# A graph layer on one core: GpSimd starts a group's gathers only after the previous group's have landed

## The reference

```
for l in range(2):
    xn = layernorm(x);  pos = xn @ Wpos + bpos + deg * Wdeg + bdeg;  xp = xn + pos
    q, k, v = (xp @ W + b) for Wq, Wk, Wv          # 8 heads of 16
    att   = clip(sum(q[dst] * k[src]) / 4, -50, 50)
    alpha = softmax of att over the edges of one dst
    x = x + segment_sum(v[src] * alpha, dst) @ Wo + bo
    x = x + gelu(layernorm(x) @ W1 + b1) @ W2 + b2
out = layernorm(x_in + x)
```

## Time and profile before

| what | value |
|---|---|
| median of 3 runs | 2100.44 us (2098.3 to 2102.22) |
| profiled execution: span from first to last instruction | 3221.0 us |
| PE busy / DVE busy / ACT busy / POOL busy in it | 1677.5 / 1445.7 / 910.1 / 1486.6 us |
| indirect DMAs on GpSimd | 1564, 1482.8 us, 948 ns each |
| moved by the gathers' queue (q0) | 205.10 MB |
| granted TensorE clock, mean | 0.694 |

### The profile page before, as it was taken

How to read it: one execution, slowest core, us unless ns; L and a number is a source line. 1 busy time by engine, 2 the same in 40 slices (tenths; PEclk the granted TensorE clock), 3 DMA queues, 4 the chain that set the end, 5 groups by cost and what they waited for, 6 DMA issues and landing times.

```text
span 3221.0 us, 44116 instructions
## 1 busy us (share of the span) xinstructions
PE 1677.5 (52%) x11693; PEld 1432.5 (44%) x11694; DVE 1445.7 (45%) x2484; ACT 910.1 (28%) x1616; POOL 1486.6 (46%) x1584
## 2 busy tenths in 40 slices
PE   7444444355566556555343534444456565556545
PEld 5344334345455445444333433343445454545444
DVE  8634434344444535454363434343444444434435
ACT  3212212123333323332131212122233233323322
POOL 0545444545444444544534445444544444444452
PEclk9667676767666777775666767676677667666667
DMA  2423333323323333333323333233333333333332
GB/s 74 136 85 109 95 99 97 105 93 113 97 95 105 108 99 96 114 105 97 116 72 101 102 95 107 90 102 98 102 103 104 103 93 98 110 98 99 101 119 75
DMA packets 120301, 322.97 MB, mean 100 GB/s; under 512 B 31459, under 2 KB 43684, under 8 KB 120170
## 3 DMA queue, kind: packets, MB, share of 16 engines
q0 software_dynamic: 75072, 205.10, 21.5%
q1 hardware_dynamic: 44292, 115.07, 10.7%
q10 hardware_dynamic: 838, 1.60, 0.2%
HBM read 313.45 MB, written 9.73 MB: 100 GB/s over the span
## 4 chain that ended last, share of the span: by engine, by line
another core or an unknown queue 29%; DVE 21%; issue 20%; PE 15%; DVEq 11%; ACT 2%; ACTq 0%; DMA 0%; POOL 0%; POOLq 0%
PE ps L1352 8%; DVE dots L1082 5%; DVEq L359 4%; PE ps L1337 4%; DVE msg L1106 4%; DVE prod L1072 3%; DVEq L393 2%; DVE hot L992 1%; DVEq L992 1%; DVE acc L987 1%; PE ps L1314 1%; DVEq L987 1%; DVE not_nan L1084 1%; DVE q_parts L839 1%
## 5 line engine op out<-in xcount | busy, mean ns | idle before, releaser
L566 POOL DMA_INDIRECT kv<-kv_tab,src_idx x1564 | 1482.8, 948 | 1697.8 <-DVE msg L1106 1131.3
L1352 PE MATMUL ps<-msg,hot 128*128 128x136 f32 x3896 | 783.3, 366 | 766.4 <-DVE acc L987 459.0
L1352 PEld LDWEIGHTS ps<-msg,hot 128*128 128x128 f32 x3896 | 705.0, 264 | 827.5 <-issue 531.8
L1337 PE MATMUL ps<-q_parts,hotT 128*128 x5844 | 545.4, 251 | 608.3 <-issue 436.6
L1337 PEld LDWEIGHTS ps<-q_parts,hotT 128*128 x5844 | 449.5, 113 | 717.5 <-issue 700.3
L1072 DVE TENSOR_TENSOR prod<-kv,ps 128x1024 f32<-128x1024 f32 (+1 forms) x198 | 238.1, 1202 | 608.3 <-remote 431.3
L705 ACT ACTIVATE hotT<-dist 128x1024 bf16 x246 | 259.9, 1057 | 535.0 <-remote 388.1
L992 DVE SCALAR_TENSOR_TENSOR hot<-dst_col,neg_base,ps 128x1024 f32<-128x1024 f32 (+1 forms) x246 | 311.8, 1267 | 144.4 <-issue 141.0
L702 ACT ACTIVATE dist<-dst_rows,neg_node 128x1024 bf16<-128x1024 int32 x246 | 282.4, 1148 | 146.1 <-issue 135.5
L987 DVE TENSOR_TENSOR acc<-acc,ps 128x136 f32 x246 | 71.3, 290 | 553.7 <-remote 316.1
L1082 DVE TENSOR_REDUCE dots<-prod 128x64 f32<-128x1024 f32 (+1 forms) x198 | 238.8, 1206 | 33.3 <-DVE prod L1072 24.2
(11 more groups left out here) (215 smaller groups left out, 995.4 us busy)
## 6 DMA issues: line engine op xcount, KB each, us to landing
dst_rows<-in_dst SPq DMA_DIRECT2D x194, 512.0 KB
kv<-kv_tab,src_idx POOLq DMA_INDIRECT x1564
kv_tab<-qkv SPq DMA_DIRECT2D x25, 128.0 KB
kv_tab<-qkv SPq DMA_DIRECT2D x3, 768.0 KB, 3.8
out_tab<-z SPq DMA_DIRECT2D x24, 64.0 KB
out<-out_tab SPq DMA_DIRECT2D x1, 1498.5 KB, 7.2
hot<-in_L_gnn_W SPq DMA_DIRECT2D x2, 256.0 KB
w<-in_L_gnn_W SPq DMA_DIRECT2D x2, 256.0 KB
```

The costliest lines, as they stand in the source:

```text
L566: pool.indirect_dma_start(kv[:, u, c, :], None, kv_tab[l][:, :], bass.IndirectOffsetOnAxis(ap=src_idx[:, c, at(g)], axis=0)).then_inc(kv_i ...
L1337: last = MM(qd[:, c * P:(c + 1) * P], hotT[:, bass.ds(pr % 2, 1), c * P:(c + 1) * P], q_parts[:, at(t), k * D:(k + 1) * D], start=first an ...
L1352: last = MM(agg, hot[:, u % 2, c, :], msg[:, u % 2, c, :], start=(c == 0), stop=(c == nch - 1))
```

## The change

A wait is added to GpSimd's loop: before the gathers of group g, all of group g - 1's must have landed, that is, the semaphore of its buffer must have its full count. It stands behind the wait for a free buffer. Nothing else changes: the same 1564 gathers, in the same order, into the same buffers.

```diff
@@ -562,6 +562,8 @@
                         pool.wait_ge(msg_done[l], g - SLOTS + 1)
                     elif l == 0 and g == SLOTS - 1:
                         pool.wait_ge(npair_ready, 1)
+                    if g:
+                        pool.wait_ge(kv_in[l][(g - 1) % SLOTS], 16 * (GC * ((g - 1) // SLOTS) + chunks_of(g - 1)))
                     for c in range(chunks_of(g)):
                         pool.indirect_dma_start(kv[:, u, c, :], None, kv_tab[l][:, :],
                                                 bass.IndirectOffsetOnAxis(ap=src_idx[:, c, at(g)], axis=0)).then_inc(kv_in[l][u], 16)
```

## The result

| kernel | median | runs | profiled span |
|---|---|---|---|
| before | 2099.48 us (2098.3 to 2102.22) | 4 | none at this speed |
| after | 2563.66 us (2560.73 to 2565.37) | 4 | 2561.5 us, mean granted clock 0.746 |

The ratio is 1.221 [1.2193, 1.2227]. The change costs 464 us where I forecast 345. The direction and the bound were right. The time lies 24 us above the upper end of my range.

The account below looks back on a forecast made before the run. GpSimd's gather issue was taken as the bound. 2100.4 us plus 347.8 (196 waits x 1.81 = 354.8, less 7) gave 2448, or 2434 if 14 us of compute were covered; forecast 2445, range 2380 to 2540 us.

Parts of the forecast that it names:

- sum of 2086 us: Kernel before if GpSimd never waits for a buffer: start, gathers, pauses, layer turn and end total 2086.0 us, 14.4 under the median.
- Hidden: Rival: the added wait disappears in GpSimd's idle time, no change, about 2100 us; chance 0.04.
- hidden in part: Rival: a compute-bound middle stage takes up its waits; only 100 x 1.81 = 181 us shows, 2280 us; chance 0.07.
- faster: Rival: gathers issue quicker with the queue drained each group, 2097 us at best; chance 0.01.
- Price of one wait: At a group's start, GpSimd pauses 2.11 us instead of 0.30, so each added wait costs 1.81 us.
- issue end to the last packet: First piece of a landing wait: from the last gather's issue end until its transfer's last busy slice, 1.48 us.
- last packet to the count: Second piece of a landing wait: from the transfer's last packets to its counted landing, 0.35 us.
- count to GpSimd's next start: Third piece of a landing wait: from the counted landing to GpSimd's next gather, 0.28 us.
- give-back at the turn: At each layer's last two groups, later landings remove VectorE's 3.5 us delay, twice: -7 us.
- signs I named: Profile after: group starts at least 2.1 us after last issue, releaser DMA or unknown; 1.25 us steps within groups; span nearly unchanged.
- More than forecast: Rival: at most groups the `dst_rows` load delays the last gather's landing; 2650 us, or about 2560 and more; chance 0.05.
- recording holds some engine back: Profiled execution of before: its 3221.0 us, 1.53 times the 2100.44 us median, was put down to profiling.

Follow-up runs that it names:

- e_swap4: Kernel after with its two waits swapped, landing wait written first, on a chip where before takes 2099.35 us: 2448.26 us, ratio 1.1659.
- e_lag2: Kernel before plus a wait for the landing of group g - 2, nearly always met, on a slow chip: 3180.97 us, ratio 0.9982.
- e_both: Kernel before plus landing waits before each group's first gather (landing written first) and fifth gather, on the 2099 us chip: 3065.04 us, ratio 1.4591.
- b_again: Kernel before, unchanged, built anew and profiled on a slow chip: 3183.34 us timed, profiled run 3153.3 us with a span of 3151.4.
- e_after2: Kernel after, unchanged, run on a slow chip beside the kernel before: 2660.49 us against 3181.97, ratio 0.8354.
- e_swap: Kernel after with its two waits swapped, landing wait written first, on a slow chip: 2675.1 us against 3183.34 for before, ratio 0.8402.
- e_pause4: Kernel before plus one scratch-tile write by GpSimd before every fourth gather, no landing wait, on a slow chip: 3149.84 us, ratio 0.9919.
- e_half: Kernel before gathering only four of eight chunks from group 4 on (output differs), on a slow chip: 1980.09 us, ratio 0.6231.
- e_midonly: Kernel before plus a landing wait only before each group's fifth gather, for its first four, on a slow chip: 2587.97 us, ratio 0.8131.
- e_pause8: Kernel before plus five scratch-tile writes by GpSimd at each group's start, no landing wait, on the 2099 us chip: 2463.07 us, ratio 1.1733.

## Why the prediction was wrong, and where it was right

**The bound.** Right. The sum of 2086 us named GpSimd's issue from durations alone, and the added waits came out in the time almost one for one: 464 us more, of which the trace gives 505.9 - 195 x 0.30 = 447 us to landing waits. "Hidden", "hidden in part" and "faster" were refuted on the chip of the forecast: no wait for a free buffer is left in the kernel after.

**Price of one wait.** This term failed: I took 2.11 us for the pause at a group's start, measured 2.59 us. Of its three pieces, "issue end to the last packet" and "last packet to the count" held together: 1.76 us to landing in the chain (2.71 - 0.95), VectorE starting after 1.92, forecast 1.83. (One of the two was misread: the last busy slice of the earlier trace rows ends at 130.5 us, not 130.6, so by that row it is 1.38 us in place of 1.48, and the forecast would have been 20 us lower.) The failed piece is "count to GpSimd's next start: 0.28 us". It came from the earlier trace rows. Two waits stand before that gather too, L554 for the table and L555 for `cols_read`, but there the late one is written first; ScalarE had met L555 at 23.9 us. That is the order of `e_swap4`. In the change the one written last is the one that is not met: 0.74 us. I wrote that "the waits add no issue worth counting", from groups whose one wait had long been met; `e_lag2` shows that this is true of met waits (0.305 us), and it does not carry over to a separate one that isn't. `e_swap4` is the control. The same two waits in the other order give pauses of 2.12 us and 2448 us in all. What differs is shown by the rows there: the separate wait stands 12.0 us before its gather where it is met early, and 0.72 us before it where it is the landing. What fills this 0.7 us is not shown.

**The sum of the kernel after**, term by term, against its span:

| term | forecast | measured |
|---|---|---|
| until the first gather | 87.0 | 87.0 |
| 1564 gathers | 1482.8 | 1483.4 |
| pauses within groups | 1366 x 0.30 = 409.8 | 441.0 |
| landing waits | 196 x 2.11 = 413.6 | 505.9 |
| turn of the layers (105.3 less the first wait, 82.1) | 21.0 | 23.2 |
| after the last gather (2561.5 - 2539.3 - 0.95) | 19.6 | 21.2 |
| sum | 2433.8 | 2561.7 |

The span is 2561.5. So 92.3 us of the miss are the landing waits and 31.2 us the pauses within groups. The second has two parts: 22 us in the 14 late second gathers, and 9 us because the usual pause is a little over 0.30 us, which I had rounded. In `e_swap4` the late gathers are 14 as well, but of 0.45 us: 418.4 us in place of 441.0. So this part too hangs on the order of the waits; its cause stays open. The two together are the difference between the kernel after and `e_swap4`: 90.3 + 22.6 = 112.9 us, and the medians are 115.4 apart.

The 14.4 us between my sum for before and its median stay partly open, since no trace of before at 2099 us exists: the rounding of the short pauses accounts for 6 to 9 of them.

**The give-back at the turn** (7 us) was not measured by itself; the two terms that hold it, the turn and the end, came out 2.2 and 1.6 us above the forecast. The signs I named held nearly throughout: a group starts over 2.1 us after the last issue with a DMA as the releaser (three starts of 196, behind one wait, are just under), and the steps inside a group are 1.25 us. The rise of more than 450 us, which I had tied to later landings, came without them.

**The upper end.** "More than forecast" rested on the `dst_rows` load. At group starts it is mostly not in the way, as I argued: `e_swap4` has 2.12 us in the mean, and in the kernel after the load was issued 4 to 7 us before the last gather at 176 of the 196 starts. `e_both` shows longer pauses with that load, in the middle of a group, and somewhat above the bound that I gave (3.46 us a pause, against 2.8 + 0.3). I had a cause above the forecast and gave it the upper end of the range; the cost that came was another, of the order of two waits, and had no bound in my range at all. A row that could have warned was in the trace of before: at the turn of the layers a separate wait, L408, stands just ahead of the gather of the earlier trace rows, which starts at 1660.23, 0.8 us later.

```profile
L408 POOLq EVENT_SEMAPHORE  x1: 17/17/17, 1659.4 to 1659.4; - x1
```

I had taken the whole turn as 18.9 us and not looked into it.

**The profiled execution.** Wrong. I forecast its span within 2% of 3221 us; it is 2561.5. The step that failed is "recording holds some engine back". `b_again` shows profiled and timed runs alike. I had taken two speeds of the same program for a difference between profiled and timed. The second step failed too: at the slow speed, where GpSimd idles over 1000 us, I had these pauses take the waits up and the span stay, and it fell to 2658.4 us (`e_after2`).

**What holds the kernel before on the other chips.** This was a faster case that I did not see (my rival of that name had another reason), though the trace ahead shows it. TensorE in the kernel before, slow speed (start, duration, instruction, [idle before]):

```profile
191.08 0.27 PE L1337 MATMUL ps<-q_parts,hotT 128*128 x1 [1.85 <-issue]
192.50 0.26 PE L1337 MATMUL ps<-q_parts,hotT 128*128 x1 [1.15 <-issue]
193.91 0.26 PE L1337 MATMUL ps<-q_parts,hotT 128*128 x1 [1.14 <-issue]
196.00 0.27 PE L1337 MATMUL ps<-q_parts,hotT 128*128 x1 [1.83 <-issue]
...
200.18 3.99 PE L1352 MATMUL ps<-msg,hot 128*128 128x136 f32 x16
204.97 2.09 PE L1352 MATMUL ps<-msg,hot 128*128 128x136 f32 x16 [0.80 <-DVE acc L987]
207.54 1.73 PE L1337 MATMUL ps<-q_parts,hotT 128*128 x24 [0.47 <-issue]
```

GpSimd at the same time:

```profile
195.64 0.95 POOL L566 DMA_INDIRECT kv<-kv_tab,src_idx  x1 [0.30 <-issue]
213.34 0.94 POOL L566 DMA_INDIRECT kv<-kv_tab,src_idx  x1 [16.75 <-DVE msg L1106]
```

And VectorE:

```profile
204.53 0.29 DVE L987 TENSOR_TENSOR acc<-acc,ps 128x136 f32 x1 [19.88 <-PE ps L1352]
```

While GpSimd issues 16 gathers without a stop, to 196.6 us, TensorE starts single matmuls 1.4 to 2.1 us apart, waiting for nothing that the profile shows. From 3.6 us after that it works without such gaps, and the next 24 matmuls of `gather_q` take 1.73 us. VectorE stood still for 19.88 us. The trace has 91 pauses of VectorE over 8 us, 1225 us in all, and 68 of them end 2 to 7 us after the last gather of a run. In the kernel after on a slow chip there are 7 (59 us), in `e_swap` 13 (125 us), in `e_pause4` 79 (1049 us).

TensorE's idle time before the matmuls of `gather_q` in which it waited for nothing that the profile shows ("issue"), in before at the slow speed, in the kernel after on a slow chip, and in the kernel after at 2561.5 us:

```profile
L1337 PE MATMUL ps<-q_parts,hotT 128*128 x5844 | 545.4, 251 | 608.3 <-issue 436.6 <-DVE prod L1072 131.8 <-ACT hotT L705 38.8
L1339 PE MATMUL ps<-q_parts,hotT 128*128 x5844 | 529.5, 259 | 345.9 <-issue 159.7 <-DVE prod L1074 118.9 <-ACT hotT L707 66.6
L1339 PE MATMUL ps<-q_parts,hotT 128*128 x5844 | 566.8, 274 | 556.0 <-DVE prod L1074 511.3 <-issue 26.9 <-ACT hotT L707 17.3
```

With `sum_pair`'s matmuls it is 729, 314 and 28 us. The granted clock does not tell the chips apart: the kernel after has 0.75 on both kinds, `e_both` 0.70 on the chip of 2099 us, `e_half` 0.86 on a slow one. What fits all this is that on the slow chips TensorE is held up during an unbroken run of gathers, and that the added wait breaks the run: `e_swap`, `e_midonly` and `e_after2` gain 500 to 600 us by it. That the one causes the other is my reading of these times; what TensorE lacks in those gaps is not shown. Whether a plain pause of 2 us does the same there wasn't tried (`e_pause8` ran on the other kind of chip), nor is it shown why a wait in mid-group (2580 us) beats one between groups (2660), or in what the chips differ. No chip was used in two sets, so that the speed belongs to the chip, and not to the time at which it ran, is inferred too.

## What to carry to other kernels

Here the kernel ran at the pace of the engine that issues the gathers, and the pauses of the added waits came out in the time almost in full (447 of its 464 us). In a kernel like it, measure the pause after the wait in question, and where two waits stand before one gather, try the one that will be met last written first (2.12 against 2.59 us here, 115 us in all; on the slow chips, where GpSimd is not the only bound, it gained nothing). When a profiled span is far from the timed median, run the same kernel timed beside it before explaining the gap; here both were true times. And a change may be worth the opposite on another chip: compare on the chip that counts.

## What the runs showed of the hardware that I had not expected

- The same program takes 2099 us on one chip and 3144 to 3200 us on four others, with TensorE's mean granted clock at 0.84 and 0.70. With the change they are 2564 and 2660 us, with its two waits in the other order 2448 and 2659 to 2675 us.
- An unbroken run of indirect gathers on GpSimd coincides with TensorE starting one matmul per 1.4 to 2.1 us on the slow kind of chip. TensorE's pauses that wait for nothing shown, before the matmuls of `gather_q` and `sum_pair`, are 729 us in the kernel before, 314 us with a pause of 2.6 us for the landing per eight gathers (`e_after2`), and 501 us with one of 0.5 us per four (`e_pause4`).
- In the chain of the kernel after, a gather starts 0.26 us after the landing behind one wait, and 0.74 us after it behind two of which the last is the late one.
- The row of a separate wait that is met stands eight gathers ahead of its own in `e_swap4` (12.0 us before it) and four ahead in `e_both` (7.0 us).
- In mid-group, where the broadcast load of `dst_rows` is issued within 1 us of a gather's start, the pause for its landing is 3.58 us in the mean, and 2.09 where it is not (`e_both`, 186 and 8 pauses).
- In `e_pause8` GpSimd's five writes of 128 x 256 numbers take 2.01 us, 0.35 us each (342.2 us for 980 of them over the whole run).
